# Token numbers as integers in the sorted rows, scatters that index from the loaded rows, and a new order of the steps

## The reference, cut to what matters

```python
scores = jnp.einsum('bsh,eh->bse', x, gate_w)
chosen = jnp.argmax(scores, axis=-1)
onehot = jax.nn.one_hot(chosen, gate_w.shape[0], dtype=x.dtype)
expert_out = jnp.einsum('bsh,efh->bsef', x, expert_w)
return x + jnp.einsum('bsef,bse->bsf', expert_out, onehot)
```

## Time and profile before

| | |
|---|---|
| median of 3 runs | 482.61 us (478.10 to 485.48) |
| the profiled execution's own time | 484.28 us |
| its span, first to last instruction | 483.0 us |
| mean granted TensorE clock | 0.958 of full speed |
| PE busy | 426.4 us, 88% |
| DVE busy | 392.7 us, 81% |
| ACT busy | 313.2 us, 65% |
| POOL busy | 281.8 us, 58% |

### The profile page before, as it was taken

The page is one execution under the profiler, slowest core; times in us unless marked ns, Lnnn a source line. Parts: engine busy times, 40 slices in busy tenths (PEclk is TensorE's granted clock), DMA queues, the critical chain, the costliest instruction groups (busy, mean ns, idle before and its releaser), DMA issues.

```text
span 483.0 us, 11082 instructions
## 1 busy us (share of the span) xinstructions
PE 426.4 (88%) x3506; PEld 333.0 (69%) x3506; DVE 392.7 (81%) x1233; ACT 313.2 (65%) x791; POOL 281.8 (58%) x354
## 2 busy tenths in 40 slices
PE   5988999897999999988999999998689979796980
PEld 3565687675878787776868786867567767675760
DVE  4778899897889999988988988998969677775450
ACT  2545468475676948856685768766839875856562
POOL 3012225528653749877584776865508767777677
PEclk9989999999899999999998999998859999999895
DMA  7562363553645473756556365646767667657621
GB/s 224 139 176 79 100 143 91 144 120 89 178 86 154 84 198 75 201 115 152 138 149 178 65 167 144 187 119 187 248 154 211 170 210 204 208 203 234 195 91 53
DMA packets 61353, 73.20 MB, mean 152 GB/s; under 512 B 17293, under 2 KB 48206, under 8 KB 61296
## 3 DMA queue, kind: packets, MB, share of 16 engines
q1 hardware_dynamic: 51616, 46.78, 36.3%
q0 software_dynamic: 8848, 25.44, 19.7%
q10 hardware_dynamic: 832, 0.27, 0.2%
HBM read 44.19 MB, written 19.22 MB: 131 GB/s over the span
## 4 chain that ended last, share of the span: by engine, by line
PE 42%; DVE 19%; DMA 10%; POOL 9%; ACT 8%; issue 6%; SPq 5%; DVEq 0%; POOLq 0%; ACTq 0%
PE bank L525 6%; PE bank L626 5%; PE bank L1354 5%; DMA front<-in_hidden_t 4%; PE bank L546 3%; DMA y<-in_hidden 3%; PE bank L1062 2%; ACT os L1394 2%; DVE kq_in L575 2%; POOL rms L1007 2%; PE both L941 2%; SPq L258 2%; DVE st L1359 2%; POOL rstd L1047 2%; ACT junk L994 2%
## 5 line engine op out<-in xcount | busy, mean ns | idle before, releaser
L1132 POOL DMA_INDIRECT sorted_rows<-rows,index x64 | 74.1, 1158 | 33.9 <-DVE st L1359 11.7
L1399 POOL DMA_INDIRECT out<-os,xs_token x71 | 69.7, 982 | 25.1 <-issue 8.8
L525 PE MATMUL bank<-front 128*64 128x256 f32 x512 | 62.8, 400 | 10.0 <-DMA front<-in_w_kv 4.9
L575 DVE SCALAR_TENSOR_TENSOR kq_in<-shared,conv_w,kq_in 128x256 f32<-128x256 f32 x144 | 60.3, 478 | 10.4 <-ACT kq_in L566 10.3
L626 PE MATMUL bank<-front 128*128 128x256 f32 x256 | 60.4, 382 | 0.1
L525 PEld LDWEIGHTS bank<-front 128*64 128x64 f32 x512 | 38.0, 144 | 30.4 <-DMA front<-in_hidden_t 10.6
L1354 PE MATMUL bank<-shared,front 128*128 x212 | 54.1, 404 | 3.0 <-issue 1.5
L626 PEld LDWEIGHTS bank<-front 128*128 128x128 f32 x256 | 46.7, 190 | 7.5 <-issue 1.3
L1354 PEld LDWEIGHTS bank<-shared,front 128*128 128x128 f32 x212 | 40.7, 200 | 10.5 <-issue 5.1
L1054 ACT ACTIVATE rows<-y,rstd 128x256 f32<-128x256 f32 x64 | 34.3, 591 | 8.3 <-POOL rstd L1047 8.0
L843 POOL TENSOR_TENSOR small<-norms 128x8 f32<-128x8 f32 x12 | 5.3, 440 | 51.3 <-DVE norms L838 51.2
(11 more groups left out here) (225 smaller groups left out, 1168.4 us busy)
## 6 DMA issues: line engine op xcount, KB each, us to landing
front<-sorted_rows SPq DMA_DIRECT2D x71, 130.0 KB
front<-in_hidden_t SPq DMA_DIRECT2D x16, 512.0 KB, 6.0
decay<-gate_clear SPq DMA_DIRECT2D x16, 512.0 KB
y<-in_hidden POOLq DMA_DIRECT2D x16, 512.0 KB, 5.6
q<-kq_in SPq DMA_DIRECT2D x64, 64.0 KB
carry<-carry_rows SPq DMA_DIRECT2D x32, 128.0 KB, 3.3
hq<-hq SPq DMA_DIRECT2D x64, 64.0 KB
shared<-in_w_expert SPq DMA_DIRECT2D x2, 1024.0 KB, 7.8
```

The costliest lines, as they stand in the source:

```text
L525: ins = pe.matmul(halves[half(side), kind, :, :], w[:, k, kind * D:(kind + 1) * D], pairs[:, k, side, :, :], start=k == 0, stop=k == KH - 1)
L575: dve.scalar_tensor_tensor(dst, raw[g][:, kind, :, tap:tap + P], conv_w[:, kind, tap:tap + 1], dst, ALU.mult, ALU.add))
L1132: pool.indirect_dma_start(sorted_rows[:, :], bass.IndirectOffsetOnAxis(index[i3][:, b:b + 1], 0), R[:, b, :], None, bounds_check=NE * REGI ...
L1399: pool.indirect_dma_start(out[:, :], bass.IndirectOffsetOnAxis(xs_token[t % LOADS][:, i:i + 1], 0), os_[o][:, i, :], None, bounds_check=TO ...
```

## The change

The token number is written as a 32-bit integer (`token` holds all chunks, so that the bias goes), and the output scatter takes its index from column 256 of the loaded rows. The cast and its buffers go. The rows are now read until the output scatters have landed, so that the load waits for the landing of the scatters of the pair that had the buffer before, and there are seven buffers in place of six. The output scatter waits for the load's semaphore. `ORDER` is written anew, 2352 steps in place of 2388 (36 steps of the cast are gone).

```diff
-LOADS = 6
+LOADS = 7
...
-        token = sb("token", [P, G * NB])
+        token = sb("token", [P, NC, G * NB], I32)
...
+        pool_const(pool.iota(token[:, :, :], pattern=[[P, NC], [S, G * NB]], base=0, channel_multiplier=1))
...
-        mark("act", n("norm"), act.activation(R[:, :, H:H + 1], token[:, g * NB:(g + 1) * NB].unsqueeze(2), ACT.Copy, bias=float(c * P)))
+        mark("act", n("norm"), act.activation(R[:, :, H:H + 1].bitcast(I32), token[:, c, g * NB:(g + 1) * NB].unsqueeze(2), ACT.Copy))
...
-    xs_token = [sb(f"xs_token{i}", [P, 2], I32) for i in range(LOADS)]
...
-        wait("sp", f"x_tok.{t - LOADS}")
+        if t >= LOADS:
+            sp.wait_ge(s_out[t % LOADS], moved(t - LOADS))
...
-        dve.wait_ge(s_row[t % LOADS], moved(t))
-        if t >= LOADS:
-            dve.wait_ge(s_out[t % LOADS], moved(t - LOADS))
-        mark("dve", f"x_tok.{t}", dve.tensor_copy(xs_token[t % LOADS][:, 0:tiles_of(t)], xs[t % LOADS][:, 0:tiles_of(t), H:H + 1].rearrange("p i f -> p (i f)")))
-        yield
...
-            wait("pool", f"x_os{i}.{t}" if i < tiles_of(t) - 1 else f"x_os.{t}", f"x_tok.{t}")
-            pool.indirect_dma_start(out[:, :], bass.IndirectOffsetOnAxis(xs_token[t % LOADS][:, i:i + 1], 0), os_[o][:, i, :], None,
+            wait("pool", f"x_os{i}.{t}" if i < tiles_of(t) - 1 else f"x_os.{t}")
+            pool.wait_ge(s_row[t % LOADS], moved(t))
+            pool.indirect_dma_start(out[:, :], bass.IndirectOffsetOnAxis(xs[t % LOADS][:, i, H:H + 1].bitcast(I32), 0), os_[o][:, i, :], None,
```

More of the change, by code:

```diff
@@ L271, in build @@
                   (zeros[:, :], 0.0), (minus_half[:, :], -0.5),
-                  (pad_row[:, 0:H], 0.0), (pad_row[:, H:H + 1], float(NO_TOKEN)), (pad_row[:, H + 1:ROW], 0.0),
+                  (pad_row[:, 0:H], 0.0), (pad_row[:, H:H + 1].bitcast(I32), NO_TOKEN), (pad_row[:, H + 1:ROW], 0.0),
                   (one[:, :], 1.0), (routed[:, :, :], 0.0), (w_route[:, :, NE:32], 0.0)]
@@ L1427 @@
[L1427 to L1434, removed]
@@ new lines @@
+    "l0p1p0l0l0l0s0l0p1l0s1p1l0l0p1l0l0p1l0s1l0p1s0l1s1l0p2p1s0l0s0s1s1p2l0s0l1p2p2s1s0s0l0p2l0s1l1p2s0l0p2s0p4p2p2s0s0p2p2p2"
+    "p5l1s0p2p2p2p2p2p3p2p2p2l1l1p2p2r0p2l1p2l1l1p2r0r0p2p2l1r0s1l1l1l1s1l1s1l1s1l1l1s0s0r0r0s2l2r0p3s2l1p3l1p3p3s2s2l2l1s1p3"
+    "l2p3s2p3p3p3p3r0p3s2s1p3p3p3p3p3p3p3l2p3p3r0p3r1l2p3l2s1e0l2l2p3p3l2p3e0e0p2l2s2r1s3p3l2s1s3e0e0e0e0l2e0r0r1p3l2l2e0r1s3"
+    "s2s2l3s2p3p4r0l2l3s2l2p4p4s2e0s3p3p4e0p4e0e0l2p4p4p3r1r1p4l2s2e0s3l3p4p4p4p4r0r1p4p4p4p4p4p6p4p4l3p4l3e0p4p3s3p4e0e0s2s2"
@@ new lines @@
+    "l3p4l2p4s3e0e0s2r1e0l3s4r1e0l3s4e0l3l3p7e0s3r0r1e0l2l3l3e0r0e0r1l3r2e0l3l4r2p4s4s3l3s3e0e0s4r2e1l4l3l3e1e1r2p5p5l3s3p5p5"
+    "e0s3p5l3s3p5l3e0s4e1p5s3l4e0e1p5e1e1l4r2p5e1p5r2p5r2s3s4p5p5p5p5r1p5p5p5p5p5p5l4p4s4r2p5p5r3l4e1p4r2s3e0l4l4l4s5l4e1e0r2"
+    "l4s5p4e1e1r3l4l4r3p5e1e1e1l4r1s4p5r2s4r1r3p5p5l4l5s4e0l4s5p5l5l4s4r3s5e2e2e1s4r3p6e1s4e2p6r3e2e1p5s5e1s4l4l5p6e1e2p6p6p6"
+    "p6p6e2s5p6e2e0e2p6p5p6e1p6p6p6p6p6p6l5p6p6p6r2r3p5e2l4e1l5l4l5e1l5e0r3e2e1s5r3l5l5e2e1p6r4r3l5e1e1l5e2r2l5s4e1r4r4l5p6s6"
@@ new lines @@
+    "s4e2s5e2p6e1e1e2r2s6p6l5r4l5p6l5p6p6s5l5l6e3s6s5e1s5l5r3e3e2l6r4r4e3e3e2p7s5e2l6s6p7r4e2s6p7e2e3l6p7p7e3l6r3e3l5p6s5l6e3"
+    "e2l6p7r3p8e3l6p7l5p7l6e1p7p7p7s5p7p7e2p7e2p7p7p7p7s5p7p7e0r4r5e2s6l6r4e2e1s6l6e2p7l6l6r5l6e2p7r5e2l6pbe2p7e3e0p7e0e3e1l6"
+    "r4e3e0s5e1p7s7e3l7p7s6s7p7s6p7e3s6s6p7e2r5e4l6s6l6r4e3l7e4s7e4l7e4r5e3r5e3p8p8e3r4s7s6e3p8l7e3p8p8r5l7e1s7p7e4e2s6l7p8s7"
+    "p8e4p8p8e4e3e4e2p8p8p8p8p8l7p8p8e1e1p8e4p8p8p8r5e3p7e2p8s7p9l7p8l7e2l6r5e1s6r4e2r4l7p8e1e3l6r5e1e4e4e4e3l7e2l7e3r6s6e4e3"
@@ new lines @@
+    "e3e4l7r6e4l7p8e3s8e3l8r6p8l7s8p8e4l7e5s8s7p8r6s7e4s7e2l8pal7s8s8s7e5l7p9s7e5r6r5p9p9e4l8e4s8e4s7e3p9p9e5p9e3s8e5e5p9p9l8"
+    "e5l7e2e5p9r6s8l7p9r6e3p9p9p9p9p9p9p9p9p9p9e4p9l8e4r5l8e4e4e5p9p9s7p9e4r6p9r7e5e2l8e3e2l8l8e4l8e4e2e3p9l8e4e5e4p8e3e5l8r6"
+    "p9e6p9r7r7s8e5s8r5s8r6e5e3r5l8l8e6r7s7l8l9s7e5e6e5e5s8e5l9s8e4l8e5e6pal8s8e4e3r6r7e5p9papae6papap9pae6l8e6e6pas8par7l9pa"
+    "papar7e4papapapapapae6papapas9r6pap9e5l9e5e5l8pae3l8l9par6l9e5pas8l9l9s9r6l9e5r7s9e5e3s9r8r8e3e4s9r7e6l9s9e3e4e5l9e6e6l9"
@@ new lines @@
+    "l9r7e6r8r7r8e6sae5e6pas9l9l9s9lae5e4sal9lar7e5e6l9s9s9s9l9lae6r8e7r8e7e7s9pbe6e5sae7sae6pbpblae4e6r8lalae7pcpbsal9lae7pb"
+    "lapbl9e7pbpbpbs9salae7s9pbpbe5pbpapbpapblapbe7pbs9pbpbs9pbpbe4e6e6pblapae4pbr7e4e6e6pblae7r7e4e4pbr9lapbr8e6r9e5lar8pfsb"
+    "pbe6sar9e7e7sbpblbe7r9e6e7sbe7lapbe5e5e6r8e6lbr8pbe5sasbsasblae7e8e8lasasae7e6r9sbr9e7r8e7pcpesbe7pcsapce8sapcpcsblapbpc"
+    "e8r9pcpclbe8e5e8e8e5pclbpce8pcpcpcpcpcpcpcpcpce6r9e7sar8pcr9e8e7pbr8lbe7lalalblbe5r9lbe7sbe6e7lbsbrae8lbe6lbe7r9e8lbe5e7"
@@ L1463 @@
+    "x4x4x2x4x4x1x2x3x3x2x0x4x1x0x3x4x0x1x4x2x4x4x3x3x4x4x0x2x1x0x1x2x1x0x2x3x1x2x4x3x4x4x2x2x1x3x4x1x3x2x4x4x0x2x2x4x3x1x2x3"
+    "x1x4x4x1x1x2x4x2x2x4x3x0x1x3x4x0x2x2x3x2x4x1x4x1x3x4x2x2x3x4x3x2x4x2x4x0x4x2x1x1x1x4x3x2x1x3x2x4x4x2x4x2x3x3x1x2x2x2x4x2"
+    "x3x4x3x4x2x4x3x3x4x4x4x4"
 )
```

52 lines of the change are left out of this document (18 added, 34 removed).

## The result

The changed kernel takes 489.34 us (median of 4 runs, 484.13 to 491.18) where the one before takes 482.22 beside it: a ratio of 1.0132, 95% interval 1.0082 to 1.0183. It is slower by 1.3%, within the 2% that the prediction called no change, but with an interval that leaves 1 out. 480.2 had been forecast, faster than before; its own range ended at 485, the wide one at 490. Timed once more, the same kernel came to 1.0185 (1.0123 to 1.0247). Ratios leave out the runs in the chip's slower state and medians do not; where the two differ, by up to 0.8%, the ratio counts.

The account below looks back on a forecast made before the run. The second layer was taken as bound by GpSimd's issue of scatters. All terms were 0 but the gap, -2.38: 484.28 to 481.9 us profiled, 480.2 as median (1.67 lower). Own range 476 to 485, wide range 470 to 490.

Parts of the forecast that it names:

- the wide one: The range for the whole time, 470 to 490 us, from within the faster case to short of the starved one.
- the order elsewhere: Steps ahead of the first output scatter (367.3 us): moves by two places of some 460 on PE, taken as 0.
- the new order of the second layer: Padding moves behind the loads of pairs 24 and 25, so GpSimd's gap before pair 24 goes: -2.38 us.
- the landing wait: SP's loads wait for scatters to land, seven buffers: loop of 13.8 us against GpSimd's 15.4 per six pairs, cost 0.
- What bounds the kernel: Second layer: GpSimd's issue of scatters, 1.285 us each, only some 4.9 of 114.6 us idle.
- The cast and the index: 36 casts on DVE (6.1 us) hidden by GpSimd's queue, and scatters indexed from the rows still 0.98 us: 0 each.
- the rule that I weighed there: A VectorE copy within SBUF can lock GpSimd out of writing descriptors; by it the change would gain 6.1 us.
- the loads starve GpSimd: Rival at SP's landing wait: a loop of 18.2 instead of 15.4 us costs 13.5 us, 496.1 in all; chance 0.12.
- its other end: Pair 26 with long landing (5.2) and slow product: ready at 457.0 us, 1.6 of the 2.38 come back.
- a sign that I had set for being right: First output scatter within 2 us of 367.3; 360 or earlier, or 372 or later, would show it wrong.

Follow-up runs that it names:

- c3: The changed kernel, seven buffers, in the order of before, with each pair's transposes and copy behind the output step of the pair three back: 538.41 us, ratio 1.1065.
- c2: The kernel before, casts and order kept, with nine row buffers and nine small index tiles instead of six: 482.53 us, ratio 1.0010.
- a1: The changed kernel's data with seven buffers, in the order of the kernel before without its cast steps: 505.64 us, ratio 1.0446.
- d1: The changed kernel timed once more without an edit, seven buffers: 492.33 us, ratio 1.0185 to the kernel before.
- a4: The changed kernel in its new order with nine row buffers in place of seven: 486.01 us, ratio 0.9939 to the kernel before.

## Why the prediction was wrong

Three terms of the sum failed: the order elsewhere, taken as 0, cost some 4 us; the new order of the second layer, taken as -2.38, added some 3 to 4.5 us of idle time before pairs 7 to 13; and the landing wait, taken as 0, cost 1.6 to 3 us before pairs 26 and 27.

*What bounds the kernel* held: GpSimd's steps of 1.285 us, with its idle time beside them, make up the tail in all runs but c3, and what moved the time was that idle time or the first scatter.

*The cast and the index, 0 each*: the index held, 978/980/1051 ns against 968/980/1052, hand-off 0.30. The casts went and the scatters did not get shorter, so the rule that I weighed there (Trainium skill, "SBUF — State Buffer", section "SBUF: two separate sides") shows nothing here. That the cast is worth nothing is borne out by c2's tail, not by its time.

*The landing wait, 0*: wrong. Not the length of the loop failed: 13.8 us was summed, and a1's chain shows 14.09 and 16.73. The sentence "it closes over six pairs, and GpSimd needs 6 x 2.57 = 15.4 for these" failed: it allows for one pair ahead of an output, where the orders have 2.06 and 3.35 on the mean. With seven buffers and a lookahead of L pairs the loop closes over 7 - L: 4.9 pairs on the mean in the new order (12.7 us of GpSimd's work) and 3.65 in the old (9.4). Neither covers 13.8, and nine buffers cover it in both (6.9 pairs, 17.8; 5.65 pairs, 14.5). That gives the sign of each run and not the size: by 13.8, a1 would lose (13.8 - 9.4) x 29 / 3.65 = 35 us, and it lost some 22. In the changed kernel itself the wait cost what stands before pairs 26 and 27, 3.0 us and 1.6 in d1, and it came by way of the padding, not by a loop that ran dry in each turn. The rival "the loads starve GpSimd" had the right place and a threshold of 15.4 that was too high for it; its price, 13.5 us, fits neither order. The Trainium skill's rule beside it, that a wait on landing in HBM pays the receipt in full ("DMA: Bandwidth & Descriptors", section "Anatomy of one DMA — SWDGE (gpsimd) path"), agrees with a1's chain, where 2.39 to 3.25 us of a turn are landings, though no trace splits the receipt from the rest.

*The new order of the second layer, -2.38*: wrong as a whole. Pair 24's gap closed, and came back as 1.97 + 1.02 at pairs 26 and 27. The working had pair 25's load at 434.4, the padding landed at 442.0 and pair 26's load at 442.5. The terms measured: pair 18's second scatter at 434.9 instead of 430.9, its landing 3.37 instead of 2.4, the padding's landing 3.96 instead of 2.4, and the table read behind it; 448.8 in all. The slow product of pair 26, which the working had as its other end, came too. That end (1.6 of 2.38 come back) was too near. The gaps of pairs 7 to 13 I had not looked for; with 5.7 us instead of 1.2 they are the larger loss of the second layer, and with a first scatter 1.2 us later they are also why pair 18 was 4 us late. What in the order makes them was not traced.

*The order elsewhere, 0*: wrong, and with the gaps of pairs 7 to 13 the largest term: some 4 us by unit 9. The step was argued from the places near the first output scatter and from "places move little"; the early units were not read at all. The bound given, 27.6 us either way, held it; the forecast's own range did not take it in.

The sum, after the fact: -2.4 expected; instead some 4 at the start and 1 to 3.5 in the tail (115.5 and 118.1 us against 114.6). That is 5 to 8 us where the two timings give 6.4 (4.0 to 8.8) and 9.0 (6.0 to 12.0). The runs don't add up to better than 2 or 3 us: a4, with the new start and the gaps of pairs 7 to 13, should be slower than its ratio says. That the first output scatter stood within 2 us of 367.3, a sign that I had set for being right, was chance: it came at 374.5 in d1.

The fastest version shown is the changed kernel's data in the old order with nine buffers: 483.17 and 483.29 us, 0.6% faster than before both times, and 9.0 us faster than the changed kernel beside it. a4 has the same ratio, but its interval reaches 1.

## What to carry to other kernels

When a buffer's release moves from an early reader to the end of its pipeline, count how many later tiles stand ahead of that end in the in-order queues: a ring of N buffers closes over about N minus that number, not over N. Here this ordered the runs with seven, eight and nine buffers rightly, but not by size, and the one run that cut the count failed for other reasons. A new order of a hand-written schedule is a change of its own, everywhere; compare the early units in both traces, at places with the same number of instructions ahead, and test it by exchanging a prefix of the order. And a gap on the bounding queue is not closed by moving what fills it earlier, if the same gap is fed by the next late transfer.

## What the runs showed of the hardware

The 32 matmuls of unit 3's projection took 5.27 to 5.36 us in all seven traces where PE had stood still for 2.33 to 3.10 us ahead of them, and 3.67 in all eleven where it had stood still for 1.67 or less, with the granted clock of that stretch at 0.93 in the kernel after and 1.00 before. Part of them ran at 1.2 instead of 2.4 GHz: from 53.65 to 57.06 us, within that group, the granted clock in the kernel after was 0.50. So at unit 3 a wait of 2 us more for a load came with 1.7 us more of matmuls. The wait right ahead doesn't decide it alone: unit 2's 32 matmuls took 5.36 us in the kernel after behind a wait of only 0.20 us, and 5.35 before behind 0.84. No run changed the wait by itself.

The padding, whose eight issues take 4.50 us in the kernel after (4.36 before), held SP's queue there until it had landed, 3.96 us after the last issue, because a wait for it stands ahead of the next table.
